# Values padded with ones: context and softmax sums from one product, and the cross attention's keys and values made in the self attention's bank

## The reference, cut to what matters

```python
def sdpa(q, k, v, causal):
    scores = jnp.einsum('bhqd,bhkd->bhqk', q * scale, k)        # masked below the diagonal if causal
    p = jax.nn.softmax(scores, axis=-1)
    return jnp.einsum('bhqk,bhkd->bhqd', p, v)

x = rms_norm(hidden_states, ln_in_w)
mixed = jnp.where(vm, x @ v_qkv, x @ l_qkv)                     # two experts, chosen by token
q, k, v = split in 16 heads of 16 columns; q, k turned by rotary
ctx = sdpa(q, k, v, causal=True)                                # 256 tokens
hidden_states = residual + jnp.where(vm, ctx @ v_dense, ctx @ l_dense)
ci = rms_norm(hidden_states, ln_post_cross_w)
cq = heads(ci @ cq_w); ck, cv = heads(encoder_outputs @ ckv_w)  # 16 heads of 8 columns, 64 memory rows
hidden_states = hidden_states + sdpa(cq, ck, cv, causal=False) @ cdense_w
mi = rms_norm(hidden_states, ln_post_attn_w)
hidden_states = hidden_states + jnp.where(vm, v_mlp(mi), l_mlp(mi))   # silu(gate) * up @ down, 688 wide
```

## Time and profile before

| | |
|---|---|
| runs | 1348.32, 1356.5, 1357.5 us; median 1356.5 |
| the profiled execution | 1357.66 us |
| its span in the trace | 1355.7 us |
| PE busy | 1303.4 us, 96% |
| PE weight loads (PEld) busy | 1052.5 us, 78% |
| DVE, ACT, POOL busy | 756.0, 489.5, 450.9 us |
| mean granted PE clock | 0.979 of full |

### The profile page before, as it was taken

One profiled execution on the slowest core, in us unless ns is written; L12 is line 12 of the kernel. 1 busy time (PEld: TensorE's weight loads), 2 busy tenths in 40 slices (PEclk: granted clock), 3 DMA queues, 4 the chain that ended last, 5 costly groups with the idle time before them and its releaser, 6 DMA issues.

```text
span 1355.7 us, 25963 instructions
## 1 busy us (share of the span) xinstructions
PE 1303.4 (96%) x10931; PEld 1052.5 (78%) x10931; DVE 756.0 (56%) x1361; ACT 489.5 (36%) x815; POOL 450.9 (33%) x559
## 2 busy tenths in 40 slices
PE   7988899999999999999999999999899999999988
PEld 6875577887887778888888888776678778787767
DVE  4445576566666656454344554346566656666553
ACT  3333323423334233254345543433341432423321
POOL 1233443534434352221121211324434345334332
PEclk9888899999999999999999999999999999999999
DMA  9010000000001001110000000011000000000000
GB/s 324 14 63 1 1 1 2 1 2 1 2 2 48 1 6 56 56 49 1 0 1 1 1 0 1 0 44 41 2 2 1 17 2 1 2 17 2 1 16 17
DMA packets 19901, 27.29 MB, mean 20 GB/s; under 512 B 3432, under 2 KB 15552, under 8 KB 19520
## 3 DMA queue, kind: packets, MB, share of 16 engines
q1 hardware_dynamic: 19008, 24.20, 5.4%
q10 hardware_dynamic: 768, 1.26, 0.3%
HBM read 23.35 MB, written 2.10 MB: 19 GB/s over the span
## 4 chain that ended last, share of the span: by engine, by line
PE 89%; DVE 3%; ACT 3%; POOL 2%; issue 2%; DMA 0%; SPq 0%; ACTq 0%; DVEq 0%; POOLq 0%
PE bank L963 6%; PE bank L1253 5%; PE bank L1218 5%; PE bank L1107 5%; PE bank L1223 5%; PE bank L1470 4%; PE bank L1463 4%; PE bank L1427 4%; PE row_banks L1367 4%; PE row_banks L1090 4%; PE row_banks L1057 4%; PE bank L1025 3%; PE bank L956 3%; PE bank L1242 3%; PE row_banks L1062 2%; PE row_banks L1320 2%
## 5 line engine op out<-in xcount | busy, mean ns | idle before, releaser
L1829 DVE TENSOR_REDUCE room<-row_banks 128x4 f32<-128x512 f32 (+1 forms) x128 | 116.5, 953 | 20.3 <-PE row_banks L1062 19.6
L1581 ACT ACTIVATE room<-row_banks 128x1536 f32<-128x1536 f32 x64 | 92.9, 1451 | 90.2 <-PE row_banks L1090 90.0
L813 POOL TENSOR_SCALAR_AFFINE_SELECT room<-room 128x1024 f32<-128x1024 f32 x64 | 70.4, 1101 | 139.6 <-ACT room L1581 139.6
L1253 PE MATMUL bank<-room,down_w 128*128 128x256 f32 x384 | 94.1, 385 | 0.5 <-DVE room L1929 0.5
L1619 ACT ACTIVATE room<-bank 128x256 f32<-128x256 f32 x96 | 36.2, 383 | 129.6 <-PE bank L1223 126.8
L1843 DVE RECIPROCAL room<-room 128x256 f32<-128x256 f32 x32 | 55.9, 1748 | 45.4 <-ACT room L1587 45.4
L1253 PEld LDWEIGHTS bank<-room,down_w 128*128 128x128 f32 x384 | 69.3, 190 | 13.3 <-issue 3.9
L834 POOL TENSOR_TENSOR room<-room,is_vis 128x192 f32<-128x192 f32 x80 | 44.8, 560 | 102.6 <-DVE room L1915 102.2
L1912 DVE SCALAR_TENSOR_TENSOR room<-room,bank 128x256 f32<-128x256 f32 x96 | 40.0, 416 | 63.7 <-ACT room L1619 63.6
L1090 PE MATMUL row_banks<-room 32*128 32x256 f32 (+1 forms) x1024 | 62.8, 360 | 9.0 <-ACT room L1581 5.3
L1090 PEld LDWEIGHTS row_banks<-room 32*128 32x128 f32 x1024 | 49.2, 192 | 26.5 <-issue 16.1
(11 more groups left out here) (244 smaller groups left out, 3051.1 us busy)
## 6 DMA issues: line engine op xcount, KB each, us to landing
out_x<-wq SPq DMA_DIRECT2D x8, 256.0 KB, 2.5
qkv<-in_L_xattn_v_qkv SPq DMA_DIRECT2D x2, 768.0 KB, 5.6
qkv<-in_L_xattn_l_qkv SPq DMA_DIRECT2D x2, 768.0 KB, 8.6
gate_w<-in_L_xattn_v_gate SPq DMA_DIRECT2D x2, 640.0 KB, 7.5
gate_w<-in_L_xattn_l_gate SPq DMA_DIRECT2D x2, 640.0 KB, 7.2
up_w<-in_L_xattn_v_up SPq DMA_DIRECT2D x2, 640.0 KB, 5.8
up_w<-in_L_xattn_l_up SPq DMA_DIRECT2D x2, 640.0 KB, 6.1
down_w<-in_L_xattn_v_down SPq DMA_DIRECT2D x2, 640.0 KB, 6.1
```

Of the source, the lines that this page charges most:

```text
L813: pool.affine_select(out=diagonal, in_=diagonal, compare_op=ALU.is_ge, fill=0.0, base=0, pattern=[[0, 8], [1, P]], channel_multiplier=-1)\
L1253: return pe.matmul(ff_bank[0][:, t * S:(t + 1) * S], down_w[:, f, t * P:(t + 1) * P], hid[:, i, :], start=(i == t == 0), stop=(i == UPS - ...
L1581: act.activation(probs[w % 2], row_banks[:, :, 0:3 * P], ACT.Exp).then_inc(*ATT_ACT.does(e, f"exp{w}"))
L1829: last = dve.tensor_reduce(dst, row_banks[:, :, P * i:P + S * i], X, ALU.max, negate=True)
```

## The change

`v_pad` and the cross attention's `cv_pad` are filled with ones where they held zeros. One product of a head then gives its context in its own 16 rows and its sums in the other 16. The two halves of a quad no longer add up: each has its own 256 columns of the bank. ACT copies the first half of the bank twice, each time multiplied with a mask of the rows wanted (`cd`, `cn`; `C_KEEP`), and DVE adds the other half under the other mask (`merge`: `md`, `mn`). The sums then stand 16 rows away from their contexts, and a shuffle on DVE (`SWAP`) brings them over before the reciprocal. Cross attention has the same with `cross_out` (`vd`, `vn`) and `cross_context`. `memory` writes to `att_bank` after the item's last merge (`mn1`), `dense` no longer waits for `cv3`, and `n0_sum` of item e+3, and `turn_max` and `a_center` where they are next on the bank, wait for `cv3` where they waited for `co1`. All four lists of `ORDER` are new. Small tiles move (`causal_f`, `media_u8` into `room`), and POOL fills the pads after the table of constants has arrived.

```diff
                     elif w == 2:
-                        pe.wait_ge(*ATT_ACT.did(e, "co0"))
-                    half = const[:, C_HALF + 32 * par:C_HALF + 32 * par + 32]
-                    for at, of_sums in ((0, False), (S, True)):
-                        for i in range(TT):
-                            for j in range(4):
-                                last = pe.matmul(att_bank[32 * j:32 * j + 32, at + i * P:at + S],
...
+                        pe.wait_ge(*ATT_DVE.did(e, "mn0"))
+                    out = att_bank[:, par * S:(par + 1) * S]
+                    for i in range(TT):
+                        for j in range(4):
+                            last = pe.matmul(out[32 * j:32 * j + 32, i * P:S], v_pad[e % 2][:, i, 8 * t + 2 * j + par, :],
+                                             probs[w % 2][:, j, S * i:S + P * i], start=(par == i == 0), stop=(par == i == 1),
+                                             skip_group_check=True)
...
                 def memory(e):
...
+                    pe.wait_ge(*ATT_DVE.did(e, "mn1"))
+                    mem = ctx_t[:, e % B * M:(e % B + 1) * M]
+                    pe.matmul(att_bank[:, 0:M], ckv_w[:, 0:C], mem, start=True, stop=True)
...
+                def dense_out(e):
+                    if e > 0:
                         pe.wait_ge(*CRS_DVE.did(e - 1, "py"))
...
-                    pe.wait_ge(*CRS_DVE.did(e, "cv3"))
...
-                    act.copy(ctx_raw[t], att_bank[:]).then_inc(*ATT_ACT.does(e, f"co{t}"))
+                    for half, name in ((1, "cd"), (0, "cn")):
+                        act.activation(ctx_raw[t][:, half * S:(half + 1) * S], att_bank[:, 0:S], ACT.Copy,
+                                       scale=const[:, C_KEEP + half:C_KEEP + half + 1]).then_inc(*ATT_ACT.does(e, f"{name}{t}"))
+
+                def cross_out(e):
+                    act.wait_ge(*CRS_PE.did(e, "cpv"))
...
+                    for half, to, name in ((1, c_sums, "vd"), (0, c_ctx, "vn")):
+                        act.activation(to, crs_bank[:, 0:S], ACT.Copy, scale=const[:, C_KEEP + half:C_KEEP + half + 1])\
+                           .then_inc(*CRS_ACT.does(e, name))
...
+                def other_half(half, raw, bank):
+                    return dve.scalar_tensor_tensor(raw, bank[:, S:2 * S], const[:, C_KEEP + 1 - half:C_KEEP + 2 - half], raw,
+                                                    ALU.mult, ALU.add)
+
+                def merge(e, t):
+                    dve.wait_ge(*ATT_ACT.did(e, f"cn{t}"))
+                    for half, name in ((1, "d"), (0, "n")):
+                        other_half(half, ctx_raw[t][:, half * S:(half + 1) * S], att_bank).then_inc(*ATT_DVE.does(e, f"m{name}{t}"))
...
+                    dve.stream_shuffle(turned, ctx_raw[t][:, S:2 * S], SWAP).then_inc(*ATT_DVE.does(e, f"turn{t}"))
+                    dve.wait_ge(*ATT_DVE.did(e, f"turn{t}"))
+                    dve.reciprocal(turned, turned).then_inc(*ATT_DVE.does(e, f"rec{t}"))
...
-                    dve.reciprocal(c_recip, crs_bank[:, S:2 * S]).then_inc(*CRS_DVE.does(e, "crec"))
+                    for half, to, name in ((1, c_sums, "d"), (0, c_ctx, "n")):
+                        other_half(half, to, crs_bank).then_inc(*CRS_DVE.does(e, f"m{name}"))
...
+                    dve.stream_shuffle(c_turned, c_sums, SWAP).then_inc(*CRS_DVE.does(e, "turn"))
```

More of the change, by code:

```diff
@@ L298 @@
[L298 to L301 removed]
+        second_scores.0.2 values.0.1 second_scores.0.3 values.0.2 first_scores.1.0 values.0.3 first_scores.1.1
@@ new lines @@
+        cross_first.1 turn_max.2 up.0.2 second_scores.2.0 up.0.3 second_scores.2.1 values.2.0 second_scores.2.2
+        cross_turn_max.1 values.2.1 up.0.4 second_scores.2.3 up.0.5 values.2.2 values.2.3 cross_second.1 down.0.0
+        memory.2 cross_values.1 down.0.1 down.0.2 first_scores.3.0 down.0.3 cross_project.1 q.4 crs_sum.1.1
+        first_scores.3.1 down.0.4 crs_spread.1.1 down.0.5 first_scores.3.2 k.4 v.4 dense.2 up.1.0 up.1.1 crs_sum.2.0
+        first_scores.3.3 crs_spread.2.0 up.1.2 n0_sum.5 cross_q.2 up.1.3 n0_spread.5 cross_first.2 up.1.4 turn_max.3
@@ new lines @@
+        up.2.2 turn_max.4 up.2.3 second_scores.4.0 up.2.4 second_scores.4.1 cross_turn_max.3 values.4.0
+        second_scores.4.2 values.4.1 second_scores.4.3 up.2.5 values.4.2 values.4.3 cross_second.3 down.2.0 memory.4
+        cross_values.3 down.2.1 down.2.2 first_scores.5.0 down.2.3 cross_project.3 q.6 crs_sum.3.1 first_scores.5.1
+        crs_spread.3.1 down.2.4 down.2.5 first_scores.5.2 k.6 v.6 dense.4 n0_sum.7 first_scores.5.3 up.3.0 crs_sum.4.0
+        up.3.1 crs_spread.4.0 up.3.2 cross_q.4 n0_spread.7 up.3.3 cross_first.4 up.3.4 turn_max.5 up.3.5
@@ new lines @@
+        second_scores.5.0 late_up.3.0 second_scores.5.1 values.5.0 late_up.3.2 second_scores.5.2 values.5.1
+        cross_turn_max.4 second_scores.5.3 late_up.3.1 cross_second.4 values.5.2 values.5.3 down.3.0 cross_values.4
+        down.3.1 down.3.2 down.3.3 down.3.4 down.3.5 cross_project.4 late_down.3.0 late_down.3.1 late_down.3.2
+        memory.5 first_scores.6.0 crs_sum.4.1 q.7 crs_spread.4.1 k.7 v.7 first_scores.6.1 dense.5 first_scores.6.2
+        up.4.0 crs_sum.5.0 first_scores.6.3 crs_spread.5.0 up.4.1 cross_q.5 cross_first.5 up.4.2 turn_max.6 up.4.3
@@ new lines @@
+        second_scores.12.3 up.10.5 cross_second.11 values.12.2 values.12.3 cross_values.11 down.10.0 down.10.1
+        down.10.2 memory.12 first_scores.13.0 cross_project.11 down.10.3 q.14 down.10.4 crs_sum.11.1 v.14
+        crs_spread.11.1 first_scores.13.1 down.10.5 dense.12 k.14 first_scores.13.2 up.11.0 crs_sum.12.0 n0_sum.15
+        up.11.1 n0_spread.15 up.11.2 crs_spread.12.0 first_scores.13.3 cross_q.12 up.11.3 cross_first.12 turn_max.13
+        up.11.4 up.11.5 second_scores.13.0 late_up.11.0 second_scores.13.1 values.13.0 cross_turn_max.12
@@ L1069, in turn_max @@
                         pe.wait_ge(*N0_DVE.did(e + 2, "y"))
[L1070 to L1071 removed]
+                    else:
+                        pe.wait_ge(*CRS_DVE.did(e - 1, "cv3"))
                     for t in range(KT):
```

712 lines of the change are left out of this document (348 added, 364 removed).

## The result

| | median of runs (lowest to highest) | profiled execution | its span | mean clock |
|---|---|---|---|---|
| before | 1354.88 us (1348.32 to 1358.06, 6 runs) | 1357.66 | 1355.7 | 0.979 |
| after | 1339.72 us (1338.81 to 1340.03, 6 runs) | 1339.94 | 1338.0 | 0.985 |

The ratio is 0.9887, with a 95% interval of 0.9864 to 0.9910: 1.1% faster, 15.2 us between the medians. The forecast was 1339.0.

What follows compares the result with a forecast made beforehand. PE was taken to bound the kernel: 1357.66 less 56.7 us of removed work, plus 21.0 of waits in the score banks' loop and 18.2 of other waits, gave 1340.2, or 1339 for the median; range 1316 to 1357.

Steps and rivals of the forecast that it cites:

- The loop of the score banks: Between second scores, PE needs 1.73 us of other work or waits for `exp`; shorter `values` lose 21.0 us there.
- cross_second to cross_values: PE needs 2.06 us of other work between these stages; halved `values` leave it short in 12 items, loss 6.1 us.
- cross_values to cross_project: The chain between these stages grows from 2.33 to 4.8 us, short in 11 items, loss 9.8 us.
- The tally: Count of PE's waits from the order lists, stage by stage; outside the score banks' loop its classes sum to 21.4 us.
- the factor 0.85: Share of the counted waits that PE really waited in the earlier trace; it cuts 21.4 us to 18.2.
- The work removed, and the rest: PE loses 56.7 us of products with ones; waits at other places in the lists cost a net 5.5 us.
- The orders: New order lists: gains of 1.5 us for `memory` off the path to `dense` and 1.4 for `first_scores` after `maximum`.
- At nothing: Parts given no cost, among them the new orders of the first and third layer (1 to 3 us if not).
- B: Rival: only the score banks' loop costs anything, the longer cross chain being covered; 1321 us, range 1310 to 1326, chance 0.15.
- C: Rival: DVE's strictly ordered list, or the bank waiting for the merge, gives the time; 1350 to 1362 us, chance 0.25.
- A: The forecast's own sum, with 0.6 to 1.2 times the waits outside the loop; 1326 to 1350 us, chance 0.50.
- D: Rival: new waits make PE's clock fall in every item's loop, slower than before; 1387 us, chance 0.08.

Runs made afterwards that it cites:

- e1: The kernel before, in its own order, with the self attention's products with ones left out and no merges: 1337.97 us, ratio 0.9891.
- e5: The kernel after with the matmuls of `values` of parts 0 and 1 issued twice: 1346.68 us, ratio 0.9959.
- e2: The kernel after with both attentions' products as before, without merges, keeping the new order and banks: 1359.74 us, ratio 1.0056.
- e11: The kernel before, in its own order, with the products with ones of both attentions left out and no merges: 1335.77 us, ratio 0.9866.
- e7: The kernel after without the merges and shuffles: 1331.43 us, ratio 0.9844.
- e9: The kernel after with the self attention's `exp` cut in two, second scores kept in their order: 1340.89 us, ratio 0.9912.

## Why the prediction was right

*The loop of the score banks.* The mechanism is right (e1, e5), the size was too large. Forecast: a loss of 21.0, and a row of some 25 us, about 28 times. Measured: 20.0 us, 31 times, 14.7 more than before; and e5, which puts the PE work of these spaces back, finds 21.1 - 7.0 = 14.1 us of cover in them. A loss of 14 to 15.

*cross_second to cross_values.* Forecast 6.1 x 0.85 = 5.2, measured 5.1 - 1.7 = 3.4.

*cross_values to cross_project.* The chain was put at 4.8 us; in item 15 it takes 1295.59 (the start of `cross_values` and its 0.87) to 1300.28, 4.7. The waits were 2.60 in item 15 (forecast 3.1) and 1.17 in item 13 (2.4: there `cross_values` itself came 1.22 late, and `values.14.3` waited 0.40 for `select` inside the chain). With both, the row grew by 5.0 (from the 1.2 of the earlier trace rows) instead of 8.3. The tally counted two waits of one item in full where the first covers for the second; the factor 0.85 was too high.

*The work removed, and the rest.* 56.7 was forecast, and PE's busy time fell by 54.1. The two are nearer than they should be, since part of the 54.1 is the clock: e2 and the kernel after, at 0.986 and 0.985, are 48.6 apart. Its idle time grew by 36.5, forecast 39.2: 14.7, 3.4 and 5.0 as above, 3.3 for `shift_q`, and 10 in rows of 0.2 to 3 us each, forecast 4.7.

*The orders.* At nothing stood those of the first and third layer. For the third this was right: its rows of L1367 (L1371 after) reach from 519.3 to 837.0 us before and from 508.8 to 826.4 after, 317.7 and 317.6. For the first, the kernel after took 110.3 us up to item 0's `turn_max` and e11, with the old order, 109.7, both at 0.95. The step that failed is the price of the new orders of the second and fourth layer. They were given 2.9 us of gain together with the bank; e2 has them at 5.1 of cost with the old products, 7 to 11 at the same clock. 3.3 of it are the row for `shift_q`, a wait that the prediction doesn't name. It was offset by the products, worth 20.0 where the forecast's terms for them come to 15.4 (10 + 5.5), and by the clock. What the new order costs or brings with the new products isn't known: the old order with them (merges put into DVE's list) wasn't tried on the chip.

*The clock, in no term.* The sum starts from an execution at 0.979 and takes its clock over unchanged; the kernel after ran at 0.985. So the change itself brought 9 to 13 us where 17.5 was summed, and the clock gave the rest. **That 1339.0 met 1339.7 is in good part luck**; the direction and the mechanism of the loop are not.

*The rivals.* B fell with the rows above: the loop is not alone. C: merges cost 8.3 by the medians, about 12 at the same clock (e7), which is what A's terms for the chain and the bank hold for them, and no more. The rule from the Trainium skill, TensorEngine Tiling (Array Packing), section PSUM Bottleneck, says that copying out may become the bottleneck; here `values` waited for a merge 1.4 us in all, so for this bank it didn't come out, while the score banks, emptied by `exp`, are such a bottleneck. D: the mean clock rose. But e9 shows that such falls exist, at 5.0 and 1.6 us, and they are as large as the effects that were to be measured.

## What to carry to other kernels

Compare runs at the same granted clock, or a stretch that has clock 1.00 in both kernels: here the clock made 9 to 13 us look like 15, hid a gain of 5 in e9, and made the price of an order look like 5 where it is 7 to 11. Before counting a removed instruction as gain, find the shortest interval that its neighbours keep whatever stands between them (here 2.60 us from one second scores to the next), and count only what exceeds it. Put the same work back at two places to see which of them had slack: 21 us cost 7 in one and 13 in the other, without any model. A shrinking row of waits proves nothing until the busy row of the same instruction has been looked at, and an order is to be priced by itself, with the old instructions in it.

## What the runs showed of the hardware

The same kernel, before the change, took 1357.2 to 1358.5 us in 18 runs at a mean clock of 0.979 and 1348.1 to 1349.1 in eight runs at 0.985 or 0.986; the thirteen at 0.984 took 1352.7 to 1353.5. Four matmuls (eight records) over two score banks took as long to reach ACT (1.05 us) as eight over four (0.99). Two activations over 128x768 took 1.51 us, one over 128x1536 1.45, so cutting `exp` in two cost ACT only 0.06. A shuffle of 128x256 took 440 to 444 ns where 380, about half of the 731 of the earlier trace rows, was forecast. And the granted clock, after the same 2.02 busy us in 3.40, fell in one kernel and not in another.
